# GpSimd fills a spare buffer and waits for it between its groups of row transfers

## The reference

```python
xn = _layernorm(x, axis=-1)
x = x + attn(xn, ...) + ffn(xn, Wr, W1, W2)
# attn: causal convolution with 4 taps, two gates, a linear recurrence over time,
#       a projection and an RMS norm
# ffn: each token goes to the expert of 8 with the highest score
xe = xf[dispatch]                                   # up to 512 tokens an expert
h = jnp.maximum(jnp.einsum('ecd,edf->ecf', xe, W1), 0.0)
ye = jnp.einsum('ecf,efd->ecd', h, W2)
ye = ye * (pe * valid.astype(ye.dtype))[:, :, None]
y = y.at[dispatch.reshape(-1)].add(ye.reshape(E * cap, d))
```

## Time and profile before

| | us |
|---|---|
| median of 3 runs | 130.79 (130.65 to 130.9) |
| profiled execution | 131.15 |
| its span (first to last instruction) | 129.3 |
| mean granted TensorE clock, of full speed | 0.931 |
| busy: TensorE / VectorE / ScalarE / GpSimd | 105.5 / 95.9 / 92.1 / 82.3 |

### The profile page before, as it was taken

How to read it: one execution, slowest core, us unless ns; L and a number is a source line. 1 busy time by engine, 2 the same in 40 slices (tenths; PEclk the granted TensorE clock), 3 DMA queues, 4 the chain that set the end, 5 groups by cost and what they waited for, 6 DMA issues and landing times.

```text
span 129.3 us, 2081 instructions
## 1 busy us (share of the span) xinstructions
PE 105.5 (82%) x676; PEld 85.9 (66%) x676; DVE 95.9 (74%) x215; ACT 92.1 (71%) x211; POOL 82.3 (64%) x107
## 2 busy tenths in 40 slices
PE   4999999999799999999999999999999996100000
PEld 4998987743369559748938989899699995000000
DVE  6488859899899981380195289999998779966670
ACT  2469699764688479879969999979971977706540
POOL 8966793057878876887877878777778787400000
PEclk9999999999999999999999999999999999755555
DMA  3993899921446173412531442111121111169995
GB/s 65 318 290 78 324 413 409 407 79 41 100 171 201 55 213 87 176 37 49 160 104 41 104 160 66 53 48 49 52 66 43 41 61 61 43 191 280 352 308 166
DMA packets 14362, 19.27 MB, mean 149 GB/s; under 512 B 1680, under 2 KB 10128, under 8 KB 14352
## 3 DMA queue, kind: packets, MB, share of 16 engines
q1 hardware_dynamic: 7968, 12.65, 29.8%
q0 software_dynamic: 2048, 4.20, 10.8%
q10 hardware_dynamic: 4336, 2.30, 6.8%
HBM read 10.76 MB, written 8.39 MB: 148 GB/s over the span
## 4 chain that ended last, share of the span: by engine, by line
PE 57%; DMA 9%; ACT 8%; POOL 8%; DVE 7%; issue 5%; SPq 2%; POOLq 1%; DVEq 0%; ACTq 0%
PE bank L558 17%; PE bank L492 9%; POOL xn_tok L384 5%; DMA dec<-y_rows 5%; PE bank L545 5%; PE bank L547 4%; PE bank L546 4%; PE bank L424 4%; ACT sq L722 3%; PE bank L574 3%; PE bank L412 3%; PE bank L532 3%; DMA xn_tok<-xn_rows,idx_in 2%; PE bank L518 2%; DMA y_rows<-xn_tok,idx_out 2%
## 5 line engine op out<-in xcount | busy, mean ns | idle before, releaser
L384 POOL DMA_INDIRECT xn_tok<-xn_rows,idx_in x32 | 33.6, 1049 | 15.9 <-issue 9.4
L391 POOL DMA_INDIRECT y_rows<-xn_tok,idx_out x32 | 31.8, 994 | 10.1 <-issue 9.7
L558 PE MATMUL bank<-w_raw,h_sb 128*128 128x128 f32 x256 | 29.9, 275 | 0.0
L558 PEld LDWEIGHTS bank<-w_raw,h_sb 128*128 128x128 f32 x256 | 29.2, 192 | 0.0
L708 ACT ACTIVATE h_sb<-bank 128x512 f32<-128x512 f32 x32 | 18.9, 597 | 4.8 <-PE bank L547 2.8
L492 PE MATMUL bank<-xc,par 128*128 128x512 f32 x32 | 15.5, 603 | 0.0
L545 PE MATMUL bank<-xg_hi,w_split 128*128 128x512 f32 x32 | 14.3, 448 | 0.3 <-ACT h_sb L708 0.3
L910 DVE TENSOR_TENSOR w_split<-w_raw,w_split 128x512 fp32r<-128x512 f32 x8 | 5.5, 690 | 11.6 <-ACT w_split L653 11.6
L547 PE MATMUL bank<-xg_hi,w_split 128*128 128x512 f32 x32 | 12.6, 394 | 0.0
L546 PE MATMUL bank<-xg_lo,w_split 128*128 128x512 f32 x32 | 12.6, 392 | 0.0
L936 DVE SCALAR_TENSOR_TENSOR xc<-xnT,par,xc 128x1020 f32<-128x1020 f32 (+2 forms) x9 | 11.5, 1277 | 0.3
(11 more groups left out here) (117 smaller groups left out, 202.7 us busy)
## 6 DMA issues: line engine op xcount, KB each, us to landing
w_raw<-in_weights SPq DMA_DIRECT2D x8, 512.0 KB, 3.6
y_rows<-sca SPq DMA_DIRECT2D x4, 512.0 KB, 5.8
dec<-y_rows SPq DMA_DIRECT2D x8, 256.0 KB, 5.3
xn_rows<-xn_tok SPq DMA_DIRECT2D x3, 512.0 KB, 4.9
x_tok<-in_x SPq DMA_DIRECT2D x4, 256.0 KB, 6.0
x_tok<-in_x ACTq DMA_DIRECT2D x2, 512.0 KB, 7.8
out<-dec SPq DMA_DIRECT2D x4, 256.0 KB, 4.0
out<-dec ACTq DMA_DIRECT2D x4, 256.0 KB, 3.4
```

Of the source, the lines that this page charges most:

```text
L384: g.indirect_dma_start(gathered[:, s * D:(s + 1) * D], None, xn_rows, bass.IndirectOffsetOnAxis(ap=idx_in[:, s:s + 1], axis=0)).then_inc(g ...
L391: g.indirect_dma_start(y_rows, bass.IndirectOffsetOnAxis(ap=idx_out[:, s:s + 1], axis=0), gathered[:, s * D:(s + 1) * D], None).then_inc(s ...
L558: last = mm(tile_of(e, s), h_sb[:, k * CAP + s * P:k * CAP + (s + 1) * P], w_raw[:, e, F + k * D:F + (k + 1) * D], start=(k == 0), stop=(k ...
```

## The change

GpSimd gets a helper `rest`: it fills the buffer `pad` (128 partitions, 512 columns of f32, read by nobody) with zeros and then waits for the semaphore `rested` that this fill raises. It is called after each group of four gathers in the first loop, and in the second loop after each group of scatters and of gathers, except behind the last scatters: 4 + 8 + 3 = 15 times.

```diff
+        pad = sb("pad", [P, 512])
...
+        rested = sem("rested")
...
             pool.wait_ge(idx_done, 1)
+            rests = [0]
+
+            def rest():
+
+                g.memset(pad[:, :], 0.0).then_inc(rested, 1)
+                rests[0] += 1
+                pool.wait_ge(rested, rests[0])
+
             AHEAD = 4
             for e in range(AHEAD):
                 gather(e)
+                rest()
             pool.wait_ge(idx_done, 2)
             pool.wait_ge(zero_out, 16 * C)
             for e in range(E):
                 scatter(e)
                 if e + AHEAD < E:
+                    rest()
                     gather(e + AHEAD)
+                if e + 1 < E:
+                    rest()
```

## The result

The changed kernel took 139.26 us (138.78 to 139.32, 3 runs) against 130.79 (130.65 to 130.9) before: a ratio of 1.0629, 95% interval 1.0589 to 1.067, slower by 8.5 us. The profiled execution took 139.32 us with a span of 137.5; before it was 131.15 with 129.3, so the two traces differ by 8.2 us.

A forecast was written before the change was run, and what follows sets the result against it. GpSimd's transfer stream, without slack beside TensorE's of about equal length, was taken to set the end. 15 rests at 0.83 us (12.45) plus 0.6 for second waits gave 13.05 us: 130.79 + 13.05 = 143.8, own range 141.0 to 146.7, wider 136.5 to 151.4.

The forecast's parts named there:

- the signs that the prediction set itself: GpSimd: fills of 0.55 to 0.6 us, 1.0 to 1.3 us across a rest, last scatter at about 124, end stretch 18.5.
- the rival with the hidden gap: GpSimd's rests: the 0.30 us gap hides in the rest, 15 x 0.38 = 5.7 us, time 136.5; chance 0.12.
- The chain of before, read literally: GpSimd has slack, only the rest ahead of the second group counts: 0.9 us, time 131.7; chance 0.05.
- The fill: GpSimd, each rest: filling 512 columns takes 0.58 us, extrapolated from fills of one and 128 columns.
- The gap of 0.30 us: GpSimd, between transfer and fill: paid once 0.68 us a rest, paid twice 0.98; middle 0.83 taken, 12.45 us for 15.
- The second wait before a scatter: GpSimd, eight rests directly before a scatter that has its own wait: 0 to 1.2 us, 0.6 taken.
- The State Buffer page's rule on the shared pair of ports: GpSimd's fills beside VectorE: a VectorE operation in 2-port mode could make a fill wait, high side only; given no term.
- TensorE's stalls and cover: TensorE's last two groups: late gathers stall it 3.6 and 3.8 us, covered by 5 us before GpSimd's last scatter group.
- The clock: TensorE in the stalls: clock falls to half throughout, adds 12.3 us, 7.5 us more at the end, 151.3; chance 0.08.
- The rival "not slower": GpSimd: the fill runs beside the transfer before it, time 130.8, at most down to 126.8; chance 0.05.

The follow-up runs named there:

- r10: Changed kernel with the first 11 rests filling 1024 columns and the 4 behind the last gathers 2048: 148.23 us beside 131.14 for the kernel before.
- r11: Changed kernel with 60 short rests of 180 columns, one after every transfer but the last four, instead of 15 long ones: 146.11 us beside 131.14 before.
- r12: Changed kernel with its 15 rests filling 768 columns instead of 512: 142.14 us beside 131.14 for the kernel before.
- e3: Changed kernel with its 15 rests filling 1024 columns instead of 512: 145.96 us, on a chip of the slow kind.
- e1: Changed kernel with all 15 fills but no wait behind each, only one ahead for the fill two rests earlier: 147.65 us beside 152.19 before.
- e6: Kernel before, without rests and without the four scatters of expert 0: 159.82 us beside 153.16 for the kernel before.
- r8: Kernel before, unchanged, traced once more on a slow chip: 154.13 us.

## Why the prediction was right, and where its size was off

By the signs that the prediction set itself, the mechanism came true and the price did not. A rest costs 0.52 us, outside the 0.68 to 1.1 it named as the sign of being wrong; across a rest it is 0.82 us from transfer to transfer, not 1.0 to 1.3, and the last scatter starts at 119.5, not about 124. The fill (0.545 us) and the end (18.0 us instead of 18.5) are close. The time lies nearer to the rival with the hidden gap (136.5) than to the forecast (143.8), and the longer transfers, for which the sum had no term, brought it 1.3 us closer by luck.

- **GpSimd's stream has no slack and sets the end.** Shown: stream + 8.7 us and span + 8.2, and in r10, r11, r12 and e3 the time follows the sum of the rests within 1.2 us. The chain of before, read literally, would have given 131.7.
- **The fill.** 0.58 us taken, 0.545 measured: 0.5 us in all.
- **The gap of 0.30 us.** This is the term that was mis-sized. I took the middle of "paid once" (0.68 us a rest) and "paid twice" (0.98). It is paid once, and behind a fill it has shrunk to 0.17; the wait costs the 0.10 us that I took. That lies between my forecast and the rival "the gap hides in the rest" (0.38 us): less than half of it hides. 0.83 taken for a rest, 0.52 measured: 4.7 us over 15 rests, of which 0.5 are the fill's and 4.1 the gap's.
- **The second wait before a scatter.** 0.6 us taken; a scatter starts 0.28 us after the fill and a gather 0.27, so at most 0.1 us. The extra 0.30 us of the earlier trace rows ahead of the first scatter went away with the rest ahead of it, and in e1, where no wait for the fill stands there, that scatter starts 0.18 us behind the fill and the gathers 0.16 or 0.17. Behind a fill those two waits cost next to nothing.
- **Longer transfers.** Given no term, 1.3 us measured. They are longer where they meet VectorE. After, GpSimd and VectorE:

```profile
39.33 1.83 POOL L386 DMA_INDIRECT xn_tok<-xn_rows,idx_in  x1 [0.27 <-POOL pad L403]
```
```profile
29.86 3.90 DVE L950 SCALAR_TENSOR_TENSOR xc<-xnT,par,xc 128x1020 f32<-128x1020 f32 x3
40.24 0.81 DVE L946 TENSOR_SCALAR xc<-xnT,par 128x1024 f32<-128x1024 f32 x1
```

  This gather ends at 41.16, 0.11 us after VectorE's operation at 41.05. In e1 and e3 the same pair ends at 41.43 and 41.31, and at 41.37 and 41.26: again 0.12 and 0.11 us apart, though the gathers started at different times. The State Buffer page's rule on the shared pair of ports (the Trainium skill, "Who interferes with whom") would fit these three, but they don't single it out: a group of L950 ends right ahead of L946, and 0.84 us before the gather does. The first long gather of after, 1.82 us from 32.77 to 34.59, ends 0.83 us after the L950 group shown above (33.76). In e1, r12, e3 and r10 that gather starts between 32.87 and 33.44, takes 1.92 down to 1.39 us, and ends 0.82 or 0.83 us after the same group. So its end is set by VectorE's operation and not by its own start; what the two share is not shown. I had applied the rule to the fill, where no run shows it, and not to the transfers.
- **TensorE's stalls and cover.** 3.6 and 3.8 us forecast, 1.5 and 2.8 measured, because the rests were shorter; the last group's copy came 3.3 us ahead of its scatter (5 forecast).
- **The clock.** After 1.5 and 2.8 us of waiting it stayed at 2.4 GHz (1.00). In runs with longer or more rests it did fall. In r10 TensorE's waits for the last two groups are 3.4 and 3.9 us, and its windows behind the second one show half clock, 1.2 GHz:

```profile
104.00:106.00 2.00, 2.00 (x12) 2.00 (x11) 0.64 (x2) 1.22 (x5) 1.63 (x2) 0.50 0.14 41
106.00:108.00 2.00, 2.00 (x17) 2.00 (x16) 0.65 (x2) 1.03 (x5) 1.39 (x3) 0.83 0.10 33
108.00:110.00 2.00, 2.00 (x21) 2.00 (x19) 0.62 (x2) 0.00 (x0) 2.00 (x2) 1.00 0.21 66
```

  The second waits of r12 (3.6 us) and e3 (3.0) are followed by the same fall, while the first ones, 3.4 us in r10 and e3, left the clock at 1.00. In r11 the clock fell twice, behind a wait of 3.25 us and, for longer, behind one of 2.6 us, which is shorter than the 2.8 us that left it at 1.00 after the change:

```profile
106.00:108.00 2.00, 2.00 (x11) 2.00 (x11) 0.71 (x2) 1.28 (x6) 1.68 (x3) 0.50 0.22 72
108.00:110.00 2.00, 2.00 (x11) 2.00 (x11) 0.58 (x1) 0.98 (x5) 1.72 (x3) 0.50 0.11 35
```

  The length of the wait alone doesn't decide it. So the rival was nearer than 0.08 said for stalls of the length that I forecast, but its price was not: I gave it half clock for 12.3 us, and the granted clock is back at 1.00 some 3 to 6 us later. From the last group's transposes to its first finished copy it is 14.1 us in r10 (117.38 + 0.28 - 103.58) and 12.6 after (112.38 - 99.78), so 1.5 us more, and r10's copy is still 7 us early. In r11 it is 15.4 us (120.91 - 105.50), 2.8 more, and its copy is ready 1.9 us before its scatter: covered still, but barely.
- **The rival "not slower".** Its mechanism, a fill beside the transfer, is refuted: the fill starts when the transfer ends. On a chip where signals are held up the changed kernel did come out 2.0% below the kernel before (0.7 to 3.3%), by a way that I had not thought of.

Not settled: that taking work from GpSimd alone would gain nothing. e6 was to show it and ran on a chip with signals held up. No version beat both kernels on both kinds of chip: with signals free the kernel before is best (131), with signals held up the 1024 columns are (146).

## What to carry to other kernels

A chain of waits names one of two streams that end together. Before costing an addition at nothing, read the other engine's own timeline from end to end: if every gap is the fixed one between its instructions, each addition shows in full. Price an insertion by the gaps that it replaces: behind a short instruction, part of the next one's preparation is already done. And look at the time of the kernel before on each chip before reading an experiment's ratio; here the change cost 6% on one chip and nothing, or gained a little, on another.

## What the runs showed of the hardware

- On three chips (kernel before at 152 to 154 us) ScalarE and VectorE stood idle beside unbroken runs of GpSimd's indirect transfers, with TensorE's work done: ScalarE for 5.2 us with a run of 16 transfers (r8) and 11.5 us with one of 20 (e6), until about 2 us after GpSimd stopped. Pauses of 1.24 us after every four transfers left GpSimd no waits for copies (e3). Whether the recording of the profile causes this is not shown.
- GpSimd: a fill starts without a gap behind a transfer. A transfer starts 0.30 us behind a transfer, 0.17 us behind a fill without a wait (512 columns, e1), 0.27 or 0.28 with one, for fills of 1 to 2048 columns, and 0.28 or 0.29 us after the end of a VectorE copy that it waited for (six of seven in r8). Fills took 0.12, 0.27, 0.545, 0.76, 0.97 and 1.82 us for 1, 180, 512, 768, 1024 and 2048 columns.
- Long gathers, of 1.39 to 1.94 us, which start while VectorE's two-input operations of L950 run, end 0.82 to 0.85 us after the last of them, whenever they started (after, e1, e3, r10, r12).
- TensorE's granted clock stayed at 1.00 (2.4 GHz) behind waits of 1.5 and 2.8 us (the change). Behind the last group's waits of 3.0 to 3.9 us (r12, e3, r10) it was 0.50 for 2 us and 0.72 to 0.85 for the next 2, with the engine fully busy, and then 1.00 again; in r11, behind 2.6 us, it was 0.50 for 4 us and 0.64 for the next 2. The group before had waited 3.4 us in e3 and r10, and nothing fell; in r11 it had waited 3.25 us, and the clock fell to 0.60 and 0.55 for 4 us.
